# A two-layer cross-attention and expert kernel: keys of the first layer two groups ahead, another order of the attention step

## The reference, cut to what matters

```python
x = x + tanh(g_xattn[0]) * attention0(layernorm(x), ctx, ctx)     # q = LN(x)Wq+bq, k = ctx Wk+bk, v = ctx Wv+bv; 16 heads of 8
x = x + tanh(g_ffn[0])   * top2_of_8_experts(layernorm(x))        # router, softmax, two experts a token, gelu, 128 -> 512 -> 128
x = x + tanh(g_xattn[1]) * attention1(ctx, ctx, layernorm(x))     # 8 x 8 weights shared by the heads, mask, softmax
x = x + tanh(g_ffn[1])   * adaptive_4_experts(layernorm(x))       # 1 to 4 experts a token, relu, 128 -> 256 -> 128
```

## Time and profile before

| what | value |
|---|---|
| median of three runs | 1396.92 us (1393.97 to 1402.14) |
| the profiled execution | 1402.06 us, of which the span from first to last instruction is 1400.3 us |
| PE busy, weight loads | 1155.6 us (83%), 947.0 us (68%) |
| VectorE, ScalarE, POOL busy | 900.4 us (64%), 752.5 us (54%), 541.8 us (39%) |
| mean granted TensorE clock | 0.911 of 2.4 GHz |
| chain that ended last, by engine | PE 52%, issue 15%, DVE 12%, unknown queue 11%, ACT 5% |
| busy tenths of PE, 40 slices of 35 us | 6887778876785399999996777778777778899998 |

### The profile page before, as it was taken

How to read it: one execution, slowest core, us unless ns; L and a number is a source line. 1 busy time by engine, 2 the same in 40 slices (tenths; PEclk the granted TensorE clock), 3 DMA queues, 4 the chain that set the end, 5 groups by cost and what they waited for, 6 DMA issues and landing times.

```text
span 1400.3 us, 40016 instructions
## 1 busy us (share of the span) xinstructions
PE 1155.6 (83%) x13845; PEld 947.0 (68%) x13845; DVE 900.4 (64%) x3061; ACT 752.5 (54%) x1629; POOL 541.8 (39%) x699
## 2 busy tenths in 40 slices
PE   6887778876785399999996777778777778899998
PEld 3665555655564199999995455556555556799997
DVE  4776655665565654555552377667667677998887
ACT  4876566665563055555552466555555566444443
POOL 2114443435535544444444444454444333122220
PEclk9999888988887699999998699899889899999999
DMA  6222111111100233333322111111111110000000
GB/s 184 77 79 67 57 38 41 45 33 43 49 26 31 68 95 94 94 94 94 94 72 76 32 35 34 37 36 35 35 35 34 33 31 4 9 23 22 22 22 23
DMA packets 116780, 71.89 MB, mean 51 GB/s; under 512 B 51736, under 2 KB 105240, under 8 KB 116632
## 3 DMA queue, kind: packets, MB, share of 16 engines
q1 hardware_dynamic: 108440, 53.13, 14.0%
q0 software_dynamic: 8192, 16.79, 4.0%
HBM read 45.88 MB, written 22.94 MB: 49 GB/s over the span
## 4 chain that ended last, share of the span: by engine, by line
PE 52%; issue 15%; DVE 12%; another core or an unknown queue 11%; ACT 5%; SPq 3%; POOL 2%; DMA 1%; DVEq 0%; ACTq 0%; POOLq 0%
PE ps_m L1759 9%; PE ps_p L1519 4%; PE ps_p L1644 4%; PE ps_m L1644 4%; PE ps_s L1476 3%; DVE mx L982 3%; PE ps_s L1745 3%; PE ps_s L1486 3%; PE ps_s L1746 2%; PE ps_s L1747 2%; PE ps_p L1534 2%; PE ps_s L1633 2%; PE ps_s L1632 2%; PE ps_s L1634 2%
## 5 line engine op out<-in xcount | busy, mean ns | idle before, releaser
L982 DVE TENSOR_REDUCE mx<-ps_s 128x8 f32<-128x512 f32 x256 | 170.3, 684 | 161.3 <-remote 112.8
L713 ACT ACTIVATE PT<-ps_p 128x512 f32<-128x512 f32 x320 | 188.2, 599 | 100.5 <-remote 41.3
L585 POOL TENSOR_TENSOR ve<-mv,eps 128x4 f32<-128x4 f32 x72 | 14.9, 207 | 439.8 <-DVE mv L925 439.8
L1519 PE MATMUL ps_p<-cst,Pr 128*128 128x128 f32 x1024 | 165.5, 297 | 13.7 <-issue 10.8
L797 ACT ACTIVATE Kbd<-ps_s,c 128x512 f32<-128x512 f32 x128 | 87.3, 688 | 113.4 <-PE ps_s L1634 113.4
L1519 PEld LDWEIGHTS ps_p<-cst,Pr 128*128 128x128 f32 x1024 | 134.5, 156 | 19.0 <-issue 17.2
L652 POOL DMA_INDIRECT w1a<-louts,gi x128 | 124.9, 976 | 38.6 <-issue 29.7
L1759 PE MATMUL ps_m<-xn3T 128*128 128x128 f32 x1136 | 137.9, 275 | 0.0
L576 POOL TENSOR_TENSOR spare<-spare 1x1 f32<-1x1 f32 x99 | 21.3, 215 | 290.4 <-DVE b1s L1337 151.1
L1759 PEld LDWEIGHTS ps_m<-xn3T 128*128 128x128 f32 x1136 | 132.7, 192 | 0.0
L863 ACT ACTIVATE xn3T<-ps_s,b1s 128x256 f32<-128x256 f32 x284 | 111.3, 475 | 26.1 <-PE ps_s L1747 26.1
(11 more groups left out here) (221 smaller groups left out, 2855.5 us busy)
## 6 DMA issues: line engine op xcount, KB each, us to landing
xn3T<-lists SPq DMA_DIRECT2D x71, 128.0 KB, 2.1
louts<-xn3T SPq DMA_DIRECT2D x71, 128.0 KB, 1.8
ctxg<-in_ctxT SPq DMA_DIRECT2D x32, 256.0 KB
Kbd<-in_ctxT SPq DMA_DIRECT2D x512, 8.0 KB
out<-x SPq DMA_DIRECT2D x16, 256.0 KB, 2.3
w1a<-in_L_ffn_W SPq DMA_DIRECT2D x8, 256.0 KB
w2a<-in_L_ffn_W SPq DMA_DIRECT2D x8, 256.0 KB
Pr<-in_ctxT SPq DMA_DIRECT2D x16, 128.0 KB, 2.5
```

Of the source, the lines that this page charges most:

```text
L713: return nc.scalar.activation(dst, src, ACT.Copy)
L982: V.tensor_reduce(mx[g.par][:, q, :], per_key(ps_s[:, q, :]), AX, ALU.max).then_inc(max_done, 1)
L1519: ins = turn(ps_p[:, c % 2, P * i:P * i + P], Pr[g.par][:, j // 2, col:col + P], ident)
```

## The change

In layer 0 the keys of group g+2 (before: g+1) are computed in step g, copied by ScalarE once into one tile kT, and from there 16 DMAs on SP's queue write the 8 x 256 blocks into Kbd, whose other parts POOL has cleared once. Ten of the 16 stand before the context load of g+3 and six behind it. The context load moves from g+2 to g+3 and now waits for the values of g+1. The values use bank 7 (before: bank 3). In both layers TensorE's step begins with the scores, queries come early, tokens-2 transposes late, and bank order is 0, 2, 3, 1; ScalarE's and VectorE's orders follow. `count` values of the waits follow the new order.

```diff
@@ -93,7 +90,7 @@
 BLOCKS = MAIN // RB + len(SPREAD) + len(AT_ONCE)
-ORDER = (2, 3, 0, 1)
+ORDER = (0, 2, 3, 1)
 def carry(touch, value):
@@ -394,7 +392,7 @@
...
             "XT": (xnT_ready, 1, 1),
-            "XT2": (xn2T_ready, 1, 1)}
+            "XT2": (xn2T_ready, 1, 1), "V": (v_ready, 1, 1)}
         def jobs(bank, g):
@@ -402,6 +400,8 @@
...
                 found = [("XT", g.plus(1)), ("XT2", g.plus(-3))]
+                if g.layer == 0:
+                    found.append(("V", g.plus(1)))
             return [j for j in found if j[1].real()]
@@ -423,7 +423,7 @@
...
             else:
-                pe.wait_ge(exp_done, last.count(4, q - 1))
+                pe.wait_ge(exp_done, last.count(4, q))
         def steps(eng, layer, step):
@@ -492,8 +492,27 @@
...
                 sp.dma_start(dst, src).then_inc(late_in, 16)
+            def spread_keys(g, some):
+
+                if 0 in some:
+                    if g.k == 0:
+                        sp.wait_ge(kbd_clear, 1)
+                    sp.wait_ge(k_ready, g.count(1, 1))
+                    wait(sp, s_done, g.count(4, -4))
+                for h in some:
+                    rows = slice(DK * h, DK * h + DK)
+                    sp.dma_start(Kbd[g.par][rows, :, h % 4, :],
+                                 kT[rows, :].rearrange("p (b k) -> p b k", b=4)).then_inc(spread_in[g.par], 16)
+
             def step(g):
-                if g.plus(2).real() and (g.layer or g.k >= 0):
+                if g.layer == 0:
+                    if g.plus(2).real():
+                        spread_keys(g.plus(2), range(0, 10))
+                    if g.plus(3).real() and g.k >= -1:
+                        load_ctx(g.plus(3))
+                    if g.plus(2).real():
+                        spread_keys(g.plus(2), range(10, H))
+                elif g.plus(2).real():
                     load_ctx(g.plus(2))
@@ -674,6 +693,8 @@
...
                         gather(g.plus(4))
+            nc.gpsimd.memset(Kbd[0][:, :, :, :], 0.0)
+            nc.gpsimd.memset(Kbd[1][:, :, :, :], 0.0).then_inc(kbd_clear, 1)
             nc.gpsimd.memset(mask_in, 0.0).then_inc(mask_clear, 1)
@@ -750,24 +771,24 @@
...
                                      scale=SCALES[g.layer]).then_inc(exp_done, 1)
-            def keys_queries(g):
-                act.wait_ge(kq_done, g.count(1, 1))
+            def keys(g):
+                act.wait_ge(k_done, g.count(1, 1))
+
+                if g.k:
+                    act.wait_ge(spread_in[1 - g.par], 16 * H * ((g.k - 1) // 2 + 1))
+                copy(kT[:, :], kq_bank[:, 0:GT], bcol[:, 1:2]).then_inc(k_ready, 1)
+
+            def queries(g):
+                act.wait_ge(q_done, g.count(1, 1))
                 wait(act, s_done, g.count(4, -4))
-                if g.layer == 0:
-                    copy(qT[g.par][:, :], kq_bank[:, GT:2 * GT], bcol[:, 0:1])
-                    for i in range(4):
-                        ins = nc.scalar.activation(Kbd[g.par][:, :, i, :], kq_bank[:, 0:GT].rearrange("p (b k) -> p b k", b=4),
-                                                   ACT.Identity, bias=bkm[:, i:i + 1], scale=blk[:, i:i + 1])
-                    ins.then_inc(kq_ready, 1)
-                else:
-                    copy(qT[g.par][:, :], kq_bank[:, GT:2 * GT]).then_inc(kq_ready, 1)
+                copy(qT[g.par][:, :], kq_bank[:, GT:2 * GT], bcol[:, 0:1] if g.layer == 0 else None).then_inc(q_ready, 1)
             def values(g):
...
                     act.wait_ge(v_done, g.count(1, 1))
-                    v = v_bank[:, 0:GT]
+                    v = bank7[:, 0:GT]
                 else:
@@ -809,23 +830,20 @@
...
                 now(probs_out, -1, 1)
-                now(tokens2, -3)
+                now(exps, 0, 0)
+                now(queries, 1)
+                if g.layer == 0:
+                    now(keys, 2)
                 now(probs_out, -1, 2)
...
                     now(values, 0)
-                now(probs_out, -1, 3)
                 now(exps, 0, 2)
                 now(exps, 0, 3)
-                if g.layer == 1:
-                    now(sums_out, -1)
-                    now(keys_queries, 1)
-                    now(exps, 0, 0)
-                else:
-                    now(exps, 0, 0)
-                    now(sums_out, -1)
+                now(probs_out, -1, 3)
+                now(tokens2, -3)
                 now(exps, 0, 1)
+                now(sums_out, -1)
                 if g.layer == 0:
-                    now(keys_queries, 1)
                     now(values, 1)
@@ -990,7 +1008,7 @@
...
             def high_maxima(g):
-                dve.wait_ge(max_done, g.count(4, 2))
+                dve.wait_ge(max_done, g.count(4, 3))
                 wait(dve, exp_done, g.count(4, -4))
@@ -1162,14 +1180,14 @@
...
                     now(statistics_in, 2)
+                    now(maximum, 0, 0)
+                    now(subtract, 0, 0)
                     now(maximum, 0, 2)
...
                     now(high_maxima, 0)
-                    now(maximum, 0, 0)
                     now(low_maxima, 0)
+                    now(maximum, 0, 1)
                     now(residual, -2)
-                    now(maximum, 0, 1)
-                    now(subtract, 0, 0)
                     now(subtract, 0, 1)
@@ -1212,17 +1230,17 @@
...
                     now(statistics_in, 2)
+                    now(maximum, 0, 0)
+                    now(subtract, 0, 0)
                     now(maximum, 0, 2)
...
                     now(high_maxima, 0)
-                    now(maximum, 0, 0)
                     now(low_maxima, 0)
+                    now(maximum, 0, 1)
                     now(moments, 2, 2, lnq_st, lnq_mv, xn_ready)
                     now(residual, -2)
-                    now(maximum, 0, 1)
-                    now(subtract, 0, 0)
+                    now(subtract, 0, 1)
                     now(statistics_mid, -2)
-                    now(subtract, 0, 1)
                     now(moments, -2, 0, lnf_st, lnf_mv, xn2_ready)
@@ -1453,15 +1470,16 @@
...
                 wait(pe, sub_done, g.count(2, 0))
-                pe.wait_ge(kq_ready, g.count(1, 1))
+                pe.wait_ge(q_ready, g.count(1, 1))
                 ranks_before = router_due(g, -5, 1) if g.layer == 0 else None
...
                     pe.wait_ge(rank_read, ranks_before.block(1))
+                wait(pe, exp_done, g.count(4, -1))
                 if g.layer == 0:
-                    wait(pe, exp_done, g.count(4, -3))
-                    pe.wait_ge(v_ready, g.count(1, 1))
+                    pe.wait_ge(spread_in[g.par], 16 * H * (g.k // 2 + 1))
+                    if g.plus(1).real():
+                        pe.wait_ge(k_ready, g.count(1, 2))
                 else:
-                    pe.wait_ge(exp_done, g.count(4, -2))
                     pe.wait_ge(kbd_in[g.par], g.u * (8 * (H + 1) * STEPS) + 16 * (H + 1) * (g.k // 2 + 1))
@@ -1505,7 +1523,7 @@
...
                 pr, half = c // 2, c % 2
-                pe.wait_ge(exp_done, g.count(4, 2 + 2 * half))
+                pe.wait_ge(exp_done, g.count(4, 3 + half))
                 if c == 0:
@@ -1542,24 +1560,29 @@
...
                 ins.then_inc(back_done, 1)
-            def keys_queries(g):
+            def keys(g):
+
+                wait(pe, sub_done, g.count(2, -3))
+                wait(pe, k_ready, g.count(1, 0))
+                wait(pe, q_ready, g.count(1, -1))
+                pe.wait_ge(ctx_in[g.par], g.half_count())
+                mm(kq_bank[:, 0:GT], wk[0][:, :], ctxg[g.par][:, :, 0, :], start=True, stop=True).then_inc(k_done, 1)
+
+            def queries(g):
                 wait(pe, sub_done, g.count(2, -1))
-                if g.layer == 0:
-                    pe.wait_ge(ctx_in[g.par], g.half_count())
-                    mm(kq_bank[:, 0:GT], wk[0][:, :], ctxg[g.par][:, :, 0, :], start=True, stop=True)
                 pe.wait_ge(xnT_ready, g.count(1, 1))
-                mm(kq_bank[:, GT:2 * GT], wq[g.layer][:, :], xnT[g.par][:, :], start=True, stop=True).then_inc(kq_done, 1)
+                mm(kq_bank[:, GT:2 * GT], wq[g.layer][:, :], xnT[g.par][:, :], start=True, stop=True).then_inc(q_done, 1)
             def values(g):
-                wait(pe, exp_done, g.count(4, -2))
+                bank_free(pe, 7, g.plus(-1), "V")
                 pe.wait_ge(ctx_in[g.par], g.half_count())
...
                     for i in range(2):
-                        ins = mm(v_bank[S * i:S * i + S, S * b:S * b + S].rearrange("p (j d) -> p j d", j=8),
+                        ins = mm(bank7[S * i:S * i + S, S * b:S * b + S].rearrange("p (j d) -> p j d", j=8),
                                  ctxg[g.par][:, b, 0, :], w[:, :, i, :], start=True, stop=True)
@@ -1655,29 +1678,30 @@
...
                 if g.layer == 0:
+                    if g.k == -1:
+                        pe.wait_ge(consts_done, 1)
+                        pe.wait_ge(setup_in, SETUP)
+                    now(scores, 0)
```

(27 more changed lines are left out.)

21 lines of the change are left out of this document (9 added, 12 removed).

## The result

Median 1531.95 us (four runs, 1524.09 to 1532.83) against 1399.53 (four runs, 1393.97 to 1402.32): a ratio of **1.095**, 95% interval 1.091 to 1.099. The forecast had 1416 and at most 1440. The profiled execution took 1532.83 with a span of 1531.1.

A forecast was written before the change was run, and what follows sets the result against it. Early steps were taken as a closed TensorE-VectorE loop, later ones as held by POOL's indirect DMAs. Start 22.2, early steps -11.3, scatter steps 0, second layer +8 gave +18.9 us: 1416 us, 8-in-10 range 1372 to 1440.

The forecast's parts named there:

- the nearest rows are the second layer's sixteen 8 KB loads of the same tile, 5.65 us to issue: First-layer spread: sixteen DMA issues priced like the second layer's loads, 5.65 us in all.
- the spread is the bound: Rival, chance 0.13: landing 4.0 us, early steps 10.5, scatter steps +0.5 from DMA collisions; +40 us, 1437.
- Start: First layer's first maxima: sixteen spreads behind SP's mask and late loads move them from 17.32 to 39.5, 22.2 us late.
- Early steps: First layer's eight steps before scatters: 9.5 us each instead of 10.92, 11.3 us back.
- the forecast's VectorE bound: Early first-layer steps: VectorE's own chain of 8.63 us plus 0.5 of statistics, 9.2 us a step.
- Scatter steps: First-layer steps with POOL's indirect DMAs: taken as 0 change, between a gain of 1.2 and 0.5 longer a step.
- The spread chain (8.6) is inside a 13.7 us step with 5 us to spare: First-layer scatter steps: copy, issues, context load and landing, 8.6 us, taken as covered at no cost.
- the values' move: First-layer scatter steps: values moved into the tokens' bank, said to hide behind the scores that now stand first.
- Second layer: Order change alone: later sums against an earlier release, +0.3 us for each of 27 gather steps, +8 us.
- TensorE gets little through: Steps with four indirect DMAs: TensorE taken to achieve little during a 5.8 us stretch, until 1.0 behind the fourth.
- the faster rival: Rival, chance 0.30: TensorE ready early; sixteen scatter steps at 12.46, second layer 16 us back; -24.6 us, 1372.
- the 0.55 for slower: Chance that the whole kernel measures slower than before: 0.37 + 0.13 + 0.05.

The follow-up runs named there:

- kh_like_ctx: Changed kernel with keys spread from an HBM buffer in the context's form (wide row pitch, gaps, own region per group): 1482.2 us, held series.
- kh_gapped: Changed kernel with keys spread from a small HBM buffer, gaps kept, row pitch 2 KB, reused every second group: 1564.6 us, held series.
- ctx_spread: Changed kernel with the first layer's sixteen spreads reading the context in HBM, so scores use raw context, not projected keys: 1232.38 us, quick series.
- best_try2: Changed kernel with four-copy keys, old second layer, earlier third context load, first-layer logits before values, VectorE/ScalarE reordered: 1426.73 us held, 1202.49 quick.

## Why the prediction was wrong

**The step that failed** is "the nearest rows are the second layer's sixteen 8 KB loads of the same tile, 5.65 us to issue". The issues took 11.6. I put bounds on the landing and none on the issue, on the ground that tile, bytes and runs are the same; the source isn't, and it decides (0.30 against 0.65 in kh_like_ctx and kh_gapped, which differ in the source buffer alone). The trace of before had a warning, SP's mask loads, 3.96 us each:

```profile
7.30 15.85 SPq L483 DMA_DIRECT2D xn3T<-in_mask  x4
```

The bounds of the issue should have been 0.35 and 3.96, and the rival "the spread is the bound" should have had its price from there. It had the mechanism that came true (ScalarE's copy into kT waits, the context load stands behind), at 1437, from a doubt about the landing alone.

The 130.2 us by which the second layer's last maxima come later, against the 18.9 forecast, part by part: start 27.3 (22.2), early steps 30.5 (-11.3), steps with scatters 36.4 (0), from the first layer's last group to the second layer's first 3.6 (nothing forecast), second layer 32.4 (8). The issue price carries most of the miss in the first two; a second term, the 0 for the scatter steps, failed beside it.

- **Start**, forecast 39.5: 44.6. SP reached the spreads at 28.78 (29.67 forecast), issued sixteen until 40.63 (11.85, forecast 5.65), and 3.96 later the maxima started (4.16 forecast). The structure was right, only the price was off.
- **Early steps**, 9.5: 14.7. That is 30.5 us lost in eight steps, not 11.3 gained. With the cheap source, ctx_spread needed 10.9: the gain wasn't there either (before, quick, 11.0). Its first four steps took 11.8 on average, with two waits of TensorE for the context, 6.7 us; the fifth and sixth took 9.2, the forecast's VectorE bound.
- **Scatter steps**, 0: 15.7 us in the mean of 23 and not 14.15, 36 us. "The spread chain (8.6) is inside a 13.7 us step with 5 us to spare" was wrong, since the chain takes 13.8. But how much of the 36 it costs isn't settled. In the held trace ScalarE and TensorE wait only 7.4 us in 7 waits for spreads and context in these steps. With cheap issues and the detour (kh_like_ctx, another held series) a step took 15.1; taken over, that is some 15 us for the price and 21 for the rest. In the quick series the price is the whole of it: the changed kernel waits 77 us there for spreads and context, and ctx_spread is faster than before. The forecast costed the values' move at nothing, behind the scores. In the held series it named the wrong cover: behind the values stand the logits and VectorE's copy of them, on which in turn the scores wait. In the changed kernel, between 165 and 520 us (before, from 105 to 430 us, VectorE waited 25.0 us in 23 waits for the logits):

```profile
DVE lgb L1041 <- remote: 108.0, 22, 7.9
...
PE ps_s L1494 <- DVE lgb L1041: 31.4, 11, 4.8
```

That the move causes these waits is argued, not shown. best_try2, with the logits ahead of the values again and ScalarE's four copies, took 15.2 us a step in a held series, hardly less.

- **Second layer**, +0.3 a step: +1.05. The forecast saw that the sums' copy comes 1.9 us later and gave it a third. In the held series the point is another: in five steps values_by_probs comes 7.2 us after the maxima and falls in the stream of gathers. These steps of 17.5 are 22 us over the usual 13.05, and the usual step is 0.35 over the 12.7 that four steps of before average (12.75, 12.75, 11.2, 14.1).
- **"TensorE gets little through" in a stretch of 5.8 us**: right in the held series, absent in the quick ones. The forecast held it against the faster rival. That the rival failed doesn't bear it out: where the stretch is absent, the changed kernel loses more, 170 us and not 132.
- **Direction**: the start and the second layer lose, as forecast, 59.7 us together; the 0.55 for slower rested on them. The other 70 came from parts forecast as a gain or as nothing, so the direction was right partly by luck.
- The Trainium skill's rule that I weighed (DMA: Bandwidth & Descriptors, Rules for kernel authors: small transfers are mostly overhead) spoke against the change, and the trace agrees in direction: sixteen transfers of 8 KB cost 11.6 us of issuing. Read at 2 us a transfer in turn it is refuted: 0.727 from start to start.

## What to carry to other kernels

Price a DMA's issue by a row with the same form of source and target, pitch included. Where the trace has none, its bounds are the cheapest and the dearest issue on that queue, and a chain of sixteen multiplies the doubt. When work is moved, look at what falls beside another engine's burst afterwards: here a small cast fell on POOL's addition, and values_by_probs in a stream of gathers. A loop through a single buffer has to be summed with bounds on each of its terms before it is called covered. And before a loss is put down to an order, look for a run with the same order that hasn't the loss.

## What the runs showed of the hardware

- The issue of the same 8 KB in 32 runs of 256 B took 0.30 us on SP's queue from rows 64 KB apart in HBM, 0.65 from rows 1 or 2 KB apart in a small HBM buffer, 0.69 from SBUF with or without gaps, 0.62 from SBUF with 1 KB runs on both sides. The wide rows also had a region of their own for each group.
- The same program took 1186 and 1382 to 1400 us in different series. In the held ones TensorE's results came about 1 us behind the fourth of POOL's indirect DMAs; in the quick ones they did not wait for it. A second-layer step of before: 8.8 against 12.5 us. The runs don't show what makes a series the one or the other.
- A VectorE cast of 0.14 to 0.21 us took 0.60 to 0.71 when it met POOL's addition of 0.74 us, and ended some 0.04 us behind it. VectorE's subtraction for the low part, of 0.17 us, was stretched to 0.59 in the same way; maxima beside the addition kept their 0.68.
